# A graph network's last layer: its dense rows spread over two stages instead of one

## What is computed

```python
x = _layernorm(x + _L0_gnn_ref(x, edge_attr_64, L0_gnn_W, L0_gnn_b, src, dst), axis=-1)
x = _layernorm(x + _L1_gnn_ref(x, edge_index_t, L1_gnn_kernel, L1_gnn_kernel_attention), axis=-1)
x = _layernorm(x + _L2_gnn_ref(x, edge_index, 0, ...W1l, b1, W1r, W2l, b2, W2r), axis=-1)
x = _layernorm(x + _L3_gnn_ref(x, edge_index, ...qw, kw, ln_gamma, ln_beta, out_w, out_b), axis=-1)
```

## Time and profile before

| | |
|---|---|
| median of three runs | 2853.88 us (2853.3 to 2862.41) |
| profiled execution | 2861.17 us, of which span 2859.5 us |
| busy over the span | DVE 2280.2 us (80%), PE 1851.7 us (65%), ACT 1735.6 us (61%), POOL 1698.8 us (59%) |
| granted PE clock, mean | 0.833 |
| DMA | 625.06 MB, mean 219 GB/s |

### The profile page before, as it was taken

How to read it: one execution, slowest core, us unless ns; L and a number is a source line. 1 busy time by engine, 2 the same in 40 slices (tenths; PEclk the granted TensorE clock), 3 DMA queues, 4 the chain that set the end, 5 groups by cost and what they waited for, 6 DMA issues and landing times. The chain is left out here.

```text
span 2859.5 us, 51576 instructions
## 1 busy us (share of the span) xinstructions
PE 1851.7 (65%) x9787; PEld 1368.6 (48%) x9787; DVE 2280.2 (80%) x9061; ACT 1735.6 (61%) x4459; POOL 1698.8 (59%) x1605
## 2 busy tenths in 40 slices
PE   5676766466666626777777666658886666656673
PEld 4565656344544414445455333336665555534442
DVE  7887887899999927887788688857776999888882
ACT  3554545333333316887778688864555888858885
POOL 7777777266656664333333666637776776327775
PEclk8777777789888867998899899989997888767876
DMA  6777877445444437999899788868886888734441
GB/s 202 240 245 230 256 247 236 139 79 85 79 79 84 71 52 256 350 330 325 325 338 344 248 291 291 298 216 252 265 263 211 292 295 294 264 136 160 163 160 52
DMA packets 280133, 625.06 MB, mean 219 GB/s; under 512 B 51230, under 2 KB 84649, under 8 KB 280055
## 3 DMA queue, kind: packets, MB, share of 16 engines
q1 hardware_dynamic: 207543, 523.73, 53.6%
q0 software_dynamic: 72512, 100.52, 16.1%
HBM read 342.76 MB, written 285.23 MB: 220 GB/s over the span
## 5 line engine op out<-in xcount | busy, mean ns | idle before, releaser
L1268 ACT ACTIVATE node_out<-node_in,n_shift,n_root 128x128 f32<-128x128 f32 (+1 forms) x1176 | 468.1, 482 | 85.5 <-DVE n_shift L1598 85.4
L795 POOL DMA_INDIRECT sums<-gat_sums,dst_safe_i x196 | 185.7, 948 | 306.1 <-DVE pre L2027 256.5
L916 POOL DMA_INDIRECT out_dram<-node_x2t,out_index x196 | 208.7, 1065 | 156.7 <-ACT node_x2t L1485 96.3
L803 POOL DMA_INDIRECT src_rows<-x_table,row_i x200 | 201.4, 1007 | 129.9 <-issue 52.2
L803 POOL DMA_INDIRECT sums<-x_table,row_i x192 | 193.8, 1010 | 87.3 <-issue 50.0
L1581 DVE BATCH_NORM_STATS2 n_stats<-node_in 128x6 f32<-128x256 f32 (+1 forms) x588 | 209.4, 419 | 25.4 <-DMA node_in<-y_nodes 14.2
L862 POOL DMA_INDIRECT gat_sums<-src_rows,add_idx x100 | 160.9, 1609 | 112.9 <-issue 24.7
L803 POOL DMA_INDIRECT own_rows<-in_x_dram,dst_safe_i x196 | 191.1, 975 | 59.7 <-issue 58.8
L1277 ACT ACTIVATE t_a<-ps 128x512 f32<-128x512 f32 (+1 forms) x198 | 115.8, 585 | 175.0 <-PE ps L961 167.9
L862 POOL DMA_INDIRECT gat_sums<-sums,add_idx x96 | 153.5, 1599 | 92.9 <-issue 31.7
L961 PE MATMUL ps<-ident,msg 128*128 128x128 f32 x590 | 105.3, 305 | 122.5 <-DVE msg L2111 57.4
(11 more groups left out here) (424 smaller groups left out, 6618.9 us busy)
## 6 DMA issues: line engine op xcount, KB each, us to landing
own_rows<-x_table SPq DMA_DIRECT2D x245, 256.0 KB, 3.3
node_in<-in_x_dram SPq DMA_DIRECT2D x96, 512.0 KB
x_table<-node_out SPq DMA_DIRECT2D x96, 512.0 KB
x_table<-new_rows SPq DMA_DIRECT2D x147, 256.0 KB
gat_sums<-node_x2t SPq DMA_DIRECT2D x49, 528.0 KB, 4.0
acc_dump<-acc SPq DMA_DIRECT2D x98, 264.0 KB
node_sums<-gat_sums SPq DMA_DIRECT2D x48, 528.0 KB
h_table<-node_h SPq DMA_DIRECT2D x48, 512.0 KB, 5.2
```

What stands on the lines that cost most here:

```text
L795: g_.indirect_dma_start(out=to[:, g.b, j, 0:width], out_offset=None, in_=tab, in_offset=bass.IndirectOffsetOnAxis(ap=indices(j), axis=0)). ...
L803: g_.indirect_dma_start(out=to4[g.q][:, j, 0:F], out_offset=None, in_=tab, in_offset=bass.IndirectOffsetOnAxis(ap=indices(j), axis=0)).the ...
L916: g_.indirect_dma_start(out=out[:, :], out_offset=bass.IndirectOffsetOnAxis(ap=out_index[:, t:t + 1], axis=0), in_=wide_new[:, g.b, j, :], ...
L1268: last = sc.activation(to[0:pn, g.b, j, :], rows[0:pn, g.b, j, 0:F], ACT.Identity, bias=NORM[k][2][0:pn, g.b, j:j + 1], scale=root[0:pn, j ...
```

## The change

The 49 dense tiles of the last layer no longer all lie in att1. Tiles 0 to 11 go into sage2, one with every fourth edge step; the other 37 go into att1, with three of every four steps. A third buffer for dense tiles is made out of `node_y` (its two halves take the tile and its result), with statistics in `NORM["a"]`. The loops of SP, ACT and DVE in att1 and of SP in sage2 now turn every four steps, and att1's own rows get a ring of four buffers. Three semaphores of an earlier stage (`others`, `e0`, `e1`) become one, `scored`, with three counts a step. SP's wait for the stores of the third layer's dense rows moves from the start of att1 to the start of sage2.

```diff
+SPACED = 12
...
+class Spaced(Step):
...
+    def index(self):
+        return self.of4
+
+
+class Packed(Step):
...
+    def index(self):
+        return 3 * self.of4 + (self.q + SPACED)
...
+def wait_third_free(eng, signal, g):
...
+    if isinstance(g, Spaced):
+        eng.wait_ge(signal.sem, g.index() + signal.base)
+    elif isinstance(g.of4, int) and g.of4 == 0:
+        eng.wait_ge(signal.sem, signal.base + SPACED)
+    else:
+        eng.wait_ge(signal.sem, g.index() + (signal.base - 2))
+
+
+def spaced(lag, stage):
...
+    def turn(g):
+        if g.q == 0 and not (isinstance(g.of4, int) and g.of4 >= SPACED):
+            stage(Spaced(g))
+    return (lag, turn, STEPS)
+
+
+def packed(lag, stage):
...
+    def turn(g):
+        if g.q < 3:
+            stage(Packed(g))
+    return (lag, turn, STEPS)
...
+        in3, out3 = ([ring[:, 0, :, :], ring[:, 1, :, :], node_y[:, i, :, :]] for i, ring in enumerate((node_in, node_out)))
...
             wait_all(sp, flow["sage1"]["stored"])
+            wait_all(sp, flow["nodes3"]["n_out"])
...
-            pipeline(sp, STEPS, edges((0, both), (1, dump), (4, store)))
+            pipeline(sp, STEPS, edges((0, both), (1, dump), (4, store)) + [spaced(1, load_last_nodes), spaced(5, store_last_nodes)], per=4)
...
-            pipeline(sp, DENSE_FULL, edges((0, load_own_back(L, x3_table, own_rows))) + [nodes(0, load_nodes(D, x3_table, SLOTS, "n_row"))]
-                     + edges((2, store_q)) + [nodes(2, store_nodes(D, out, 0))])
+            pipeline(sp, DENSE_FULL, edges((0, load_own4)) + [packed(1, load_last_nodes)]
+                     + edges((3, store_q)) + [packed(3, store_last_nodes)], per=4)
...
-            pipeline(act, STEPS, edges((3, new_x3), (2, root), (0, sage_copies)), per=4)
+            pipeline(act, STEPS, edges((3, new_x3), (2, root)) + [spaced(3, last_node_root)] + edges((0, sage_copies))
+                     + [spaced(3, last_node_rows(0, J)), spaced(4, last_node_rows(J, DJ))], per=4)
...
-            pipeline(act, DENSE_FULL, [nodes(1, roots(D, "n")), nodes(1, normed_rows(D, "n", node_in, node_out, "n_row", "n_out"))]
-                     + edges((1, queries_keys_out), (0, att_copies)))
+            pipeline(act, DENSE_FULL, [packed(1, last_node_root), packed(1, last_node_rows(0, DJ))]
+                     + edges((1, queries_keys_out), (0, att_copies)), per=4)
...
-            pipeline(dve, STEPS, edges((3, x3_shifts), (0, sources_landed), run[0], run[1], (2, x3_moments), run[2], run[3],
-                                       (0, means)), per=4)
+            pipeline(dve, STEPS, edges((3, x3_shifts), (0, sources_landed), run[0], run[1], (2, x3_moments), run[2], run[3], (0, means))
+                     + [spaced(3, last_inverses), spaced(3, last_shifts), spaced(2, last_more), spaced(2, last_moments)], per=4)
...
-            pipeline(dve, DENSE_FULL, edges(spread[0]) + [nodes(1, node_inverses)] + edges(spread[1]) + [nodes(1, node_shifts)]
-                     + edges(spread[2], (2, products), spread[3], (2, score_sums)) + [nodes(0, nodes_x3_more), nodes(0, nodes_x3_moments)])
+            pipeline(dve, DENSE_FULL, edges(spread[0]) + [packed(1, last_inverses)] + edges(spread[1]) + [packed(1, last_shifts)]
+                     + edges(spread[2], (2, products), spread[3], (2, score_sums)) + [packed(0, last_more), packed(0, last_moments)], per=4)
```

More of the change, by code:

```diff
@@ L77, in index, with __init__, wait_third_landed, wait_third_drained @@
         return (2 * self.k + self.b) * -1 + (STEPS - 1)
+class Spaced(Step):
+    def __init__(self, g):
+        super().__init__(g.of4, 0, g.q, g.of4)
+    def index(self):
+        return self.of4
+class Packed(Step):
+    def __init__(self, g):
+        super().__init__(g.of4, g.q, g.q, g.of4)
+    def index(self):
+        return 3 * self.of4 + (self.q + SPACED)
+class Thirds:
+    def __init__(self, ring, third):
+        full = (DENSE_FULL - SPACED) // 3
+        self.sems, self.first = [*ring.sems, third], ring.base[0]
+        self.base = [ring.base[0] + 16 * SPACED, ring.base[1], 0]
+        self.end = [self.base[0] + 16 * (full + len(TAIL_PARTS)), self.base[1] + 16 * full, 16 * full]
+def wait_third_landed(eng, t, g):
+    if is_tail(g):
+        eng.wait_ge(t.sems[0], t.end[0])
+    else:
+        eng.wait_ge(t.sems[g.b], 16 * g.of4 + ((t.first if isinstance(g, Spaced) else t.base[g.b]) + 16))
+def wait_third_drained(eng, t, g):
+    base = t.first if isinstance(g, Spaced) else t.base[g.b]
+    if base or not (isinstance(g.of4, int) and g.of4 == 0):
+        eng.wait_ge(t.sems[g.b], 16 * g.of4 + base)
+def wait_third_free(eng, signal, g):
[3 more added lines that the diff above has]
+        eng.wait_ge(signal.sem, signal.base + SPACED)
+    else:
+        eng.wait_ge(signal.sem, g.index() + (signal.base - 2))
[9 more added lines that the diff above has]
+    return (lag, turn, STEPS)
 def back(g):
@@ L506, in gnn_program @@
                 flow[layer][n] = Signal(sem(n), 0, per)
+        own_in4 = Quad([*flow["att1"]["own"].sems, *flow["sage2"]["own2"].sems],
+                       [*flow["att1"]["own"].base, *flow["sage2"]["own2"].end], 1, STEPS)
+        flow["att2"]["own"] = Ring(own_in4.sems[0:2], own_in4.end[0:2], 1, WIDE_STEPS)
+        rows_in3 = Thirds(flow["nodes4"]["n_in"], sem("n_in2"))
+        rows_out3 = Thirds(flow["nodes4"]["n_out"], sem("n_out2"))
         LAYER_NO = {n: i for i, n in enumerate(("msg", "sage1", "sage2", "att2"))}
@@ L908, in _ @@
             L = flow["att2"]
-            wait_all(pool, flow["nodes4"]["n_out"])
+            for b in range(3):
+                pool.wait_ge(rows_out3.sems[b], rows_out3.end[b])
             def scatter_rows(g):
@@ L1463, in _ @@
             L = flow["att2"]
-            wait_all(act, flow["nodes4"]["n_out"])
+            for b in range(3):
+                act.wait_ge(rows_out3.sems[b], rows_out3.end[b])
             def silu(g, jn=WJ):
@@ L1877, in add @@
                     v.scalar_tensor_tensor(to[:, g.b, j, 0:F], after, undone[:, bass.ds(back(g).index() * J + j, 1)],
-                                           rows[:, g.b, j, :], ALU.mult, ALU.add).then_inc(L["spread"].sem, 1)
+                                           own4[g.q][:, j, :], ALU.mult, ALU.add).then_inc(L["spread"].sem, 1)
                 return add
```

92 lines of the change are left out of this document (63 added, 29 removed).

## The result

The changed kernel takes **2864.35 us** (median of 20 runs, 2846.29 to 2874.76) where the kernel before takes 2853.88 (20 runs): ratio 1.0038, 95% interval 1.0023 to 1.0052. The forecast was 2842 us, faster. A second set of 11 and 25 runs gave 1.0025 (1.0004 to 1.0046). So it is slower by 0.3 to 0.4%, where a gain of 0.4% was expected.

The account below looks back on a forecast made before the run. Sage2 was taken as bound by POOL's gathers, att1 by DVE. Sage2 +13 and att1 -25 gave -12 us, from a median of 2853.9 to 2842 us; range for 8 in 10: 2825 to 2872.

Parts of the forecast that it names:

- Sage2, +13: Sage2 with 12 tiles more: DVE becomes the bound, 21.15 us a group against the gathers' 20.1, so 13 us slower.
- 4.4: DVE's own time in us for a sage2 step, without its wait for a gather and with the turn of its loop.
- 3.55: DVE's time in us for one tile in sage2: 3.1 plus 0.45 for the reciprocal and the shift.
- ACT ... has 2 us free in every step. Nothing.: Sage2: a tile adds 3.4 us to ACT in four steps, which its free time takes in; no cost.
- Rival 1: TensorE, idle about 3.4 us behind a sage2 tile, falls to half clock: sage2 +36, total 2882 us, slower; chance 0.2.
- POOL, SP, DMA: no price: Sage2: POOL's 20.6 us a group hidden by DVE, SP taken as nothing (0 to 12 us kept), DMA fits.
- Own rows are needed more than one step later: Sage2: reason why SP's own rows, queued behind a tile's load, were taken to cost nothing.
- the reserve: Sage2's DMA: share 0.81 becomes 0.97; 6.2 MB in 21.15 us, 293 GB/s, should fit.
- Att1, -25: Att1 with 12 tiles fewer: a group goes from 24.9 to 22.8 us, 25 us faster, bounds -8 and -35.
- The 1.15 us stall: Att1: after the step without a tile to load, DVE waits 1.15 us for ACT's copy before the next product.
- 2.2 for half clock: Att1: with TensorE at half clock a tile's root comes later and a group takes 2.2 us more, 24.2.
- Half clock was put at 0.8 us a group: Att1: half clock taken for 38% of the stage, 0.38 x 2.2 us on top of 22.0, giving 22.8.

Follow-up runs that it names:

- experiment 5: Changed kernel with ACT's rows of sage2's tiles thinned to one of each four, DVE, SP and DMA doing whole tiles: sage2 266.6 us.
- experiment 3: Changed kernel with ACT's tile in sage2 in pieces of 3, 3 and 2 rows instead of two of 4: sage2 269.0 us, 270.9 in a second kernel.
- experiment 9: Changed kernel with sage2's 12 tiles loaded and stored as one row of eight, all waits and instructions kept: sage2 279.1 us, ratio 1.0070.

## Why the prediction was wrong

**Sage2, +13: the step that failed.** "DVE needs 4 x 4.4 + 3.55 = 21.15 us for four steps." With ACT's rows out of the way (experiment 5) it is 21.85, and 12 x 0.7 = 8.4 us of the shortfall are this. The error is in 4.4 and not in 3.55 (2.84 + 0.73 = 3.57): a step's own time was taken as its length less its wait, 4.37, but that wait covered a gap of issue of 0.17 in each step, which appears when the wait goes, and the step is 4.53. Four times 0.16 are nearly all of the 0.7; the turn of the loop, 0.13, was in the 4.4. The stage's 266.6 less 243.1 is 23.5, so another 2 are in dumps and the first and last groups.

**"ACT ... has 2 us free in every step. Nothing."** This failed too, and cost the other 10 us, 276.6 against 266.6. The free time is there (140 of 240 us busy), but not where it is wanted: in the steps behind a tile four rows of 1.64 us stand between the copies and the edge root, and DVE comes up to 1.5 us before the root. By order alone most of it comes back (6.7 us in the mean of two profiles, experiment 3).

**Rival 1** named a right place and almost the right idle time (3.4 forecast, 2.93 at 2074) and gave 2882. The clock does fall behind a tile; only the price was off, some 4 us where it said 23 more: the falls last 3.5 to 7.2 us each, and what ends last is ACT's root, not TensorE's result. Nor does the length of one idle time decide, as this rival's reading of the earlier trace rows had it. In the changed kernel the clock is 0.50 behind 2.93 us and 0.52 behind 1.32; in the second profile of the kernel before it falls to 0.51 behind one idle time of 1.54 us and to 0.52 behind one of 1.95, while the earlier trace rows has it kept behind 2.07, and experiment 5 behind 2.62. The Trainium skill ("TensorE: Matmul & The Clock Gate", Part 1, the clock gate) has the rule that an idle array loses its clock and must earn it back. With that rule the trace agrees in that every fall seen stands behind idle time. The price is the runs' alone.

**POOL, SP, DMA: no price**, right as things stand (bytes cut to an eighth gain nothing), but for SP by luck. "Own rows are needed more than one step later" was wrong, as TensorE waited 6.9 + 4.2 us for them; it cost nothing, since experiment 9 has none of these waits and a stage as long. And the reserve is smaller than thought: with DVE and ACT relieved, waits for transfers held the stage at 260.7. A gather stretched by the tile's addition was seen 7 times in sage2, up to 1.95 us, where twelve were forecast; DVE hid them.

**Att1, -25: right**, -24 in the mean of eleven profiles. The 1.15 us stall came as worked out (13.5 us for 13, the one of 3.0 being the start), and a group that doesn't wait for the tile's root takes 22.0 us, as in the forecast. What comes on top is that root: in the second profile eight of the twelve groups wait 1.8 us for it (the forecast had 2.2 for half clock), in the first a few wait 0.6 to 0.9. Half clock was put at 0.8 us a group; 16 added transposes a step gave 3 us in all, beside 10 forecast, but in a kernel where the rows stand elsewhere.

**The passage** between the stages had no term and cost 4 to 5 us. DVE's waits in it grew by as much: 6.2 us for ACT's root of the edge norm (2.6 before) and 2.5 for the first tile to be loaded (0.4 before), against 4.5 for the tiles' roots (5.8 before). Nothing was run on it; why is open.

The sum by stages, +33.5 - 24 + 4 = +13.5 from single profiles, stands beside +10.5 by the medians.

## What to carry to other kernels

The slack of an engine is not its wait: take the step's length less the wait, and add back the issue gap that the wait covered; 0.16 us a step were 8 of the 20 us missed here. When an engine becomes the bound, ask of each other engine not how much time it has free but what stands in its queue ahead of the thing the new bound waits for. And before moving a filler, look for the round trip it fills: eight rows of ACT moved there cost 40 us, four of them saved 8.

## What was not expected of the hardware

TensorE's clock could be held up by transposes that nobody reads (0.90 to 0.97 in sage2, 0.82 to 0.99 in att1), at a gain of 4 and 3 us only. It fell behind single idle times of 1.54 and 1.95 us in one profile and was kept behind 2.07 and 2.62 in others. And cutting the tile's transfers to an eighth left the stage as long (279.1 us against 275.8 to 278.2) while DMA's load fell from 271 to 231 GB/s in the same window.
